# The second layer and the gates by time, the first unit's gates among the first layer's products, and the last pass' fourth head by token halves

## The chip, the cores and the metric

The kernel runs on one NeuronCore of a Trainium2 chip, as one program in one launch. The metric is the device time in microseconds; beside it stands the span, from the first to the last instruction of one profiled execution. Engine names are those of the profile: PE is TensorE's matrix products and PEld its weight loads, DVE is VectorE, ACT is ScalarE, POOL is GpSimd, SP is SyncE, which issues DMAs. The matrix engine writes into PSUM; ScalarE and VectorE read it from there.

## The reference

`x` is 32 x 32 tokens of 256 numbers (batch b, time t), `cond` 32 x 256. Two units are added to x one after the other.

```python
# unit 1: an adaLN block, then a minGRU over time
ada = cond @ ada_w + ada_b                      # shift1, scale1, gate1, shift2, scale2, gate2
x1  = ln(x) * (1 + scale1) + shift1
q, k, v = x1 @ qkv_w + qkv_b                    # 16 heads of 128, attention over the 32 tokens of a batch entry
y   = x + gate1 * (softmax(q k^T / sqrt(128)) v @ out_w + out_b)
h   = gelu((ln(y) * (1 + scale2) + shift2) @ ffn_w1 + ffn_b1)      # 1024 wide
y   = y + gate2 * (h @ ffn_w2 + ffn_b2)
k   = y @ Wz.T + bz ;  n = y @ Wn.T + bn        # gates; the state runs over t:
s_t = (1 - sigmoid(k)) * s_(t-1) + sigmoid(k) * g(n),   s_0 = 0.5 ;   x = x + s
# unit 2: a recurrence over t with drive x, then a sparse MLP
for t in range(32):                             # four Runge-Kutta stages each
    q, p = rk4(q, p, drive=x[:, t])             # dq = q - q^3/3 - p + drive + tanh(q) @ coupling.T + bias
r = q_trace ;  mask = top 4 of 16 blocks of r @ Wr.T + br
x = x + (gelu(r @ W1.T) * mask) @ W2.T
```

## The kernel before

All arrays are held whole in SBUF. Products that need more than half precision are made of f16 pairs, a high and a low part: three products each (high by high, low by high, high by low). ScalarE makes the high part while it empties a PSUM bank, VectorE subtracts and makes the low part, which frees the bank. PSUM is five banks (`bank`), used in turn by a numbered list of uses (`USE_...`; `bank_of` and `count_of` give a use's bank and its turn; `fill` waits for a bank to be free, `full` and `free` are the semaphores), and beside them `score` (two banks) and `spare`.

The program has these stages, and each engine has its own order of work in them, written by hand; the engines meet only in semaphores.

1. *Attention* in four passes of four heads (`attention_pass`). A pass has projections, scores, the mixing of values by the softmax (`mix`, one head each), and output projections (`out_project(pair, c, js)`, c is a quarter of the tokens, js are heads). The softmax of a head is placed as 32x32 blocks on the diagonal of `ptx`: high parts by ScalarE (`place_high`, four strips of 32x256), low parts by GpSimd (`place_low`; in the last pass VectorE has half of those of the fourth head, `place_last_low`). Mixing writes heads into `ao_sb` after `empty_pv` and `low_pv` (`low_last_pv` for the fourth).
2. *The end of the last pass.* When the heads' sums of quarters 0 and 1 are finished, VectorE takes them (`take_heads`), adds them to `acc` (`last_heads`), makes the statistics of the tokens of half 0, and a first part of them is normalised by VectorE, the rest by ScalarE. TensorE turns them (`turn_normed`, `turn_x2`), VectorE scales and shifts (`scale_turned`, `shift_turned`), ScalarE and VectorE make the pair (`x1_high`, `x1_low`). `ada_late` are small products for the modulation. `unread(dst, n)` are n products that nobody reads.
3. *The MLP and the gates.* Tokens are in two halves by batch entry (h is 0 or 1, 512 columns). `hidden_layer(h)` is the first layer, eight uses m of 512 columns, each followed by gelu and a copy on ScalarE and by a difference on VectorE (`hidden_low`). `output_layer(h)` is the second layer, two output blocks ob, 48 products of 512 columns. `residual(h)` adds it to `x3`. `gates(h)` are the f32 products for the minGRU, `min_gru` its recurrence by a scan on VectorE. For h = 1 the gates are split in time already: `EARLY` is t from 0 to 7, `LATE` the rest (`early_gru`, `late_sum`, `late_product`, `late_scan`, `late_drive`). `drive_bias` and `drive_lows` put the result into `drive_pair`, the recurrence's drive. The order on TensorE is hidden_layer(0), output_layer(0), hidden_layer(1), gates(0), output_layer(1), last_gates.
4. *The recurrence.* Eight rounds of four steps of four stages n = 0 to 15. A stage is a chain: ScalarE makes tanh of the state, first in f16 and then in f32, VectorE the low part and the cubic term, TensorE adds drive, coupling and cubic term into `score`, and the next stage's tanh reads it. Beside it TensorE has pieces of the sparse MLP of the group before (`FILL[n]`), unread products (`UNREAD_AT`), ScalarE and VectorE pieces of their own; in round 0 these are the late part of the minGRU (`first_round`), in round 1 its rest (`second_round`). TensorE's rounds are one hardware loop.

TensorE before, between the MLP and the recurrence:

```python
hidden_layer(1)
gates(0)
output_layer(1)
last_gates()
for use in (USE_GRU[1], USE_GRU[1] + 3):
    pe.wait_ge(free[bank_of(use)], count_of(use) + 1)
unread(bank[bank_of(USE_GRU[1])][:], 4)
```

Of the kernel before, what the change touches and what calls it, by code (L numbers as in the profile page):

```python
# [92 lines left out]
def build(nc, xtok, xT, condT, ada_w, vecs, gate_b, out_b, gate_rows, br, wqk, wv, wo, ffn_w1, ffn_w2, wzT, wnT, coupT, wrT, w1T, w2T, out):  # L93
    with ExitStack() as ctx:
# [121 lines left out]
        NE, NL = NBH * 2 * UNROLL, NBH * (T - 2 * UNROLL)  # L216
        parts_at = 2 * MB * P
        early_store = big[:, parts_at:parts_at + KB * 6 * NE].rearrange("p (k w n) -> p k w n", k=KB, w=6)
        parts_at += KB * 6 * NE
# [94 lines left out]
        last_taken = sem("last_taken")  # L314
        pv_full = sem("pv_full")
# [21 lines left out]
        early_full = sem("early_full")  # L337
        early_gate = sem("early_gate")
# [33 lines left out]
        USE_F1 = [[AFTER + n for n in (2, 5, 6, 3, 4, 7, 8, 9)], [AFTER + 3 * KB + MB + m for m in range(MB)]]  # L372
        USE_F2 = [AFTER + 2 * KB + MB, AFTER + 5 * KB + 2 * MB]
        USE_GRU = [AFTER + 3 * KB + 2 * MB, AFTER + 6 * KB + 2 * MB]
# [105 lines left out]
        def _(pool):  # L480
# [23 lines left out]
            for i in range(NQUAD):  # L504
                def place_low(j):

                    if j == QUAD - 1:
                        use = (LAST_PV if i == NQUAD - 1 else USE_PV)[j - 1] + 1
                        pool.wait_ge(full[bank_of(use)], i * NPAR + count_of(use))
                    for q in range(NB4 // 2 if i == NQUAD - 1 and j == QUAD - 1 else NB4):  # L510
# [11 lines left out]
            pool.wait_ge(ptx_ready, NQUAD * QUAD * NB4)  # L522
# [3 lines left out]
        def _(act):  # L526
# [5 lines left out]
            def x1_high(n):  # L532
                h = n % NH
                for k in range(KB):
                    s = slice(h * HALF, (h + 1) * HALF)
                    act.wait_ge(normed, n * KB + k + 1)
                    nc.scalar.activation(x1_pair[:, 0, k, s], drive[:, k, s], ACT.Copy).then_inc(x1_high_ready, 1)  # L537
# [44 lines left out]
            for i in range(NQUAD):  # L582
# [48 lines left out]

                def place_high(j):
# [61 lines left out]
                copy_scores(3, NB4 // 2 if last else NB4)  # L694
                place_high(2)
                exps(3)
                if not last:
                    empty_next_proj(0, 1)
                empty_pv(2, [0])
                place_high(3)  # L700
                empty_pv(2, [1])
                if last:
                    mlp_highs(5, 7)
                else:
                    for t in range(1, 4):
                        weights_high(i + 1, t)
                empty_pv(3)
                if last:
                    mlp_highs(7, 8)
                else:  # L710
# [26 lines left out]

            normalise_x2(0)
            empty_x2(0)
            x1_high(NH)  # L740
            for h in range(NH):
                for m in range(MB):
                    n = h * MB + m
                    if n == MB:
                        normalise_x2(1)
                        mlp_highs(8, 11)
                        x1_high(NH + 1)
                        empty_x2(1)
                        mlp_highs(11, 16)
                    if n >= NGELU:  # L750
                        act.wait_ge(hid_low_ready, n - NGELU + 1)
                    use = USE_F1[h][m]
                    empty(use, gelu_of[n % NGELU], ACT.Gelu, bias=v_("ffn_b1", m), scale=1.0 / WSCALE)
                    act.wait_ge(free[bank_of(use)], count_of(use) + 1)
                    nc.scalar.activation(hid_pair[:, m, 0, h * HALF:(h + 1) * HALF], gelu_of[n % NGELU], ACT.Copy
                                         ).then_inc(hid_high_ready, 1)
            act.wait_ge(coup_ready, 6)
            act.wait_ge(hid_low_ready, NH * MB - 3)
# [10 lines left out]
            def relu_pair(n, piece, cols, ob, src, ready):  # L769

                nc.scalar.activation(nneg_of[n % 2][:, cols], src[:, cols], ACT.Relu, bias=bn_neg[:, ob:ob + 1], scale=-1.0
                                     ).then_inc(gate_in, 1)
                nc.scalar.activation(nn_of[n % 2][:, cols], src[:, cols], ACT.Relu, bias=bn_twice[:, ob:ob + 1], scale=2.0
                                     ).then_inc(ready, 1)
                act.wait_ge(gate_in, piece + 1)
                nc.scalar.activation(nneg_of[n % 2][:, cols], nneg_of[n % 2][:, cols], ACT.Tanh, scale=-0.5
                                     ).then_inc(tn_ready, 1)

            def gate_tanh(n, cols, ob, ready):

                nc.scalar.activation(tz_of[n % 2][:, cols], bank[bank_of(USE_GRU[n // KB] + 2 * ob + 1)][:, cols], ACT.Tanh,
                                     bias=hb[:, ob:ob + 1], scale=0.5).then_inc(ready, 1)

            def wait_product(use):
                act.wait_ge(full[bank_of(use)], count_of(use))

            every = slice(0, HALF)

            for ob in range(KB):
                use = USE_GRU[0] + 2 * ob  # L790
                wait_product(use)
# [1658 lines left out]
```

## Time and profile before

| | us |
|---|---|
| median of 3 runs | 478.56 (478.54 to 478.62) |
| the profiled execution | 478.5 |
| its span | 476.7 |
| PE busy in the span | 464.0 |
| DVE busy | 388.2 |
| ACT busy | 316.9 |
| POOL busy | 47.5 |

The time is that of the whole execution; 1.8 us of it lie outside of the span. Times of the trace count from the first instruction. Attention ends near 228, the first hidden layer starts at 241.4, the recurrence at 300.0. Several engines are busy at once, so shares add up to more than one, and the busy time of matrix products includes the end of each, which overlaps the next one: two products that start 0.22 us apart have 0.38 us each.

### The profile page before, as it was taken

The numbers are of one execution on the slowest core, as the hardware profiler recorded it, in microseconds if no ns is written. First come the engines' busy times: TensorE is split into PE (matmuls) and PEld (weight loads), VectorE is DVE, ScalarE is ACT, GpSimd is POOL, SyncE is SP. The second block draws the span as 40 slices with busy tenths as digits, with TensorE's granted clock in tenths as the row PEclk, the third lists the DMA queues.
The fourth block names the chain that finished last, engine by engine and source line by source line (L and its number), as shares of the span: only waits on it lengthen the run. The fifth ranks groups of instructions, "written<-read, shape, count | busy, mean of one in ns | idle before, by whom it ended". The sixth has DMA issues, their size and how long they took to land.

```text
span 476.7 us, 13783 instructions
## 1 busy us (share of the span) xinstructions
PE 464.0 (97%) x5264; PEld 333.7 (70%) x5264; DVE 388.2 (81%) x1388; ACT 316.9 (66%) x951; POOL 47.5 (10%) x77
## 2 busy tenths in 40 slices
PE   7999999999999999999999999999999999999997
PEld 4455776557755776559635445889898988989886
DVE  4969885869768799998796998898888888888884
ACT  1678873788477965887566974756566656656563
POOL 3010240222120240223000000000000000000000
PEclk9999999999999999999999999999999999999999
DMA  8992511110202000000000000000000000000000
GB/s 288 419 392 71 121 46 36 43 45 23 67 1 66 22 0 2 0 2 1 1 1 1 0 1 0 3 3 1 1 11 1 11 1 11 1 11 12 0 12 23
DMA packets 10400, 20.86 MB, mean 44 GB/s; under 512 B 1472, under 2 KB 4992, under 8 KB 9728
## 3 DMA queue, kind: packets, MB, share of 16 engines
q1 hardware_dynamic: 9808, 19.89, 12.1%
q10 hardware_dynamic: 560, 0.60, 0.4%
q8 instruction: 14, 0.23, 0.2%
q14 instruction: 18, 0.15, 0.1%
HBM read 19.40 MB, written 1.08 MB: 43 GB/s over the span
## 4 chain that ended last, share of the span: by engine, by line
PE 85%; DVE 6%; ACT 4%; DMA 1%; issue 1%; POOL 1%; SPq 0%; DVEq 0%
PE bank L977 57%; PE score L977 26%; PE spare L977 2%; DMA ao_sb<-xtok 1%; POOL ptx L513 1%; ACT ptx L637 1%; ACT th L858 1%; ACT ao_sb L590 1%; DVE drive L1559 1%; ACT x L537 0%; DVE q_group L2310 0%; DVE drive L1563 0%; DVE acc L1651 0%; DVE drive L1714 0%; PE bank L1019 0%
## 5 line engine op out<-in xcount | busy, mean ns | idle before, releaser
L977 PE MATMUL bank<-x,pairs_store 128*128 128x512 f16 x384 | 86.3, 379 | 0.5 <-ACT x L537 0.4
L977 PEld LDWEIGHTS bank<-x,pairs_store 128*128 128x128 f16 x384 | 36.9, 98 | 43.4 <-issue 1.4
L513 POOL TENSOR_TENSOR ptx<-pt,ptx 32x256 f16<-32x256 f32 x62 | 43.2, 696 | 176.3 <-ACT ptx L637 172.9
L977 PE MATMUL score<-cub,neg_eye 128*128 128x64 f32 x256 | 55.6, 299 | 0.0
L590 ACT ACTIVATE big<-bank,head_b 128x512 f16<-128x512 f32 x60 | 39.8, 685 | 17.4 <-PE bank L977 17.1
L2189 DVE TENSOR_TENSOR thlo<-th 128x64 f16<-128x64 f32 x128 | 28.8, 225 | 25.2 <-ACT th L859 23.9
L977 PE MATMUL score<-th,coup_part 128*128 128x32 f16 x1024 | 46.3, 177 | 1.1
L977 PE MATMUL bank<-pairs_store,ao_sb 128*128 128x256 f16 x360 | 43.0, 273 | 0.7 <-issue 0.2
L977 PE MATMUL bank<-pairs_store,x 128*128 128x512 f16 x192 | 43.4, 379 | 0.0
L858 ACT ACTIVATE th<-score 128x64 f16<-128x64 f32 x96 | 21.4, 223 | 32.5 <-PE score L977 29.5
L977 PEld LDWEIGHTS bank<-pairs_store,ao_sb 128*128 128x128 f16 x360 | 34.0, 98 | 7.6 <-DVE ao_sb L1752 1.5
L977 PEld LDWEIGHTS score<-th,coup_part 128*128 128x128 f16 x1024 | 34.6, 96 | 5.5 <-ACT th L858 3.0
L977 PEld LDWEIGHTS score<-cub,neg_eye 128*128 128x128 f32 x256 | 38.1, 188 | 0.0
L977 PE MATMUL bank<-q_high,f_sb 128*128 128x128 f16 x288 | 36.9, 219 | 0.0
L977 PE MATMUL bank<-big,f_sb 128*128 128x128 f16 x456 | 36.3, 219 | 0.2 <-DVE big L2229 0.2
L1752 DVE SCALAR_TENSOR_TENSOR big<-bank,head_b,big 128x512 f16<-128x512 f32 x48 | 33.8, 738 | 0.3 <-ACT big L590 0.2
L977 PE MATMUL score<-thlo,coup_part 128*128 128x32 f16 x512 | 33.5, 179 | 0.3
L977 PEld LDWEIGHTS bank<-pairs_store,x 128*128 128x128 f16 x192 | 18.6, 98 | 21.1 <-issue 0.2
L977 PE MATMUL score<-drive_pair,scaled_eye 128*128 x256 | 31.3, 195 | 1.4 <-issue 0.3
L977 PEld LDWEIGHTS bank<-big,f_sb 128*128 128x128 f16 x456 | 29.2, 101 | 0.5 <-issue 0.3
L588 ACT ACTIVATE big<-bank 128x512 f16<-128x512 f32 x32 | 18.9, 593 | 15.7 <-PE bank L977 15.4
L977 PEld LDWEIGHTS score<-thlo,coup_part 128*128 128x128 f16 x512 | 24.2, 99 | 6.9
(279 smaller groups left out, 1046.7 us busy)
## 6 DMA issues: line engine op xcount, KB each, us to landing
wqk_sb<-wqk SPq DMA_DIRECT2D x16, 256.0 KB, 2.7
wv_sb<-wv SPq DMA_DIRECT2D x4, 512.0 KB, 5.4
wo_sb<-wo SPq DMA_DIRECT2D x4, 512.0 KB, 3.8
f_sb<-ffn_w SPq DMA_DIRECT2D x2, 1024.0 KB, 15.1
ao_sb<-xtok SPq DMA_DIRECT2D x4, 256.0 KB, 5.8
x_sb<-xT SPq DMA_DIRECT2D x1, 1024.0 KB, 12.4
w_sb<-w1T SPq DMA_DIRECT2D x1, 1024.0 KB, 16.0
w_sb<-w2T SPq DMA_DIRECT2D x1, 1024.0 KB, 16.9
```

The lines of the kernel that those rows point to most:

```text
L513: nc.gpsimd.tensor_tensor(ptx[s, 1, :, s], pt[s], ptx[s, 0, :, s], ALU.subtract).then_inc(ptx_ready, 1)
L588: ins = nc.scalar.activation(dst, src, ACT.Copy)
L590: ins = nc.scalar.activation(dst, src, ACT.Identity, bias=bias)
L637: nc.scalar.activation(ptx[s, 0, :, s], pt[s], ACT.Copy).then_inc(high_placed, 1)
L858: nc.scalar.activation(th16[:].rearrange("p (k b) -> p k b", k=KB), src, ACT.Tanh, scale=unit).then_inc(th16_ready, 1)
L977: return nc.tensor.matmul(dst, lhsT, rhs, start=start, stop=stop, **kw)
L1559: V.tensor_tensor(tok(drive[:, k, s]), tok(bank[turned_bank][:]), mod(SCALE1, k, h), ALU.mult).then_inc(free[turned_bank], 1)
L1752: ins = V.scalar_tensor_tensor(lo, bank[bank_of(use)][:], bias, hi, ALU.add, ALU.subtract)
L2189: V.tensor_tensor(thlo[:], th32[:], th16[:], ALU.subtract).then_inc(lo_ready, 1)
```

## The change

*Last pass.* The fourth head's scores, softmax, placing and mixing are done by token halves (`copy_half`, `exps_half`, `place_high_half`, `half_strips`, `shift_half`, `normalise_half`, `mix_half`). TensorE finishes quarters 0 and 1 of all heads first; the second half of the fourth head's mixing and the output projection of quarter 3 come after them, and the last output projections of quarters 2 and 3 go among the turning of the tokens, where unread products were. The modulated tokens of half 0 are written to `centred` instead of `drive`. ScalarE makes x1 before it copies `x3`, and all conversions of the sparse MLP's weights come before the second half's x1.

*MLP and gates.* The first gates of half 0 are made after three of the eight uses of the first layer of half 1, the second ones after all eight. The second layer of half 1 is made for `EARLY` first, into `spare`, both output blocks, then for `LATE`, each block by itself; its residual follows in the same parts, and the early gates stand among the late products of the first block. Of the late gates two products are left before the recurrence, the others are in its stages 0 to 3.

*Recurrence.* Round 0 is written out on TensorE, without logits, second-layer products of a group before and unread products; the loop has rounds 1 to 7. ScalarE's and VectorE's late pieces lie in other stages.

The diff, cut to its core:

```diff
 # TensorE, last pass
+def mix_half(j, h):
+    base = i * (QUAD * NB4) + NB4 * (j + 1)
+    late = j == QUAD - 1
+    pe.wait_ge(high_placed, base + NB4 * h if late else base)
+    dst = score[:, h] if late else fill(use_pv[j] + h)
+    (8 products with the high part of ptx, for the 4 groups of half h)
+    if late:
+        pe.wait_ge(half_placed[h], NB4)
+    else:
+        pe.wait_ge(ptx_ready, base)
+    (4 products with its low part)
 out_project(0, 0, [0, 1])
 out_project(0, 1, [0, 1])
+if last:
+    mix_half(2, 0)
+    mix_half(2, 1)
+    out_project(0, 2, [0, 1])
+    mix_half(3, 0)
+    out_project(1, 0, [2])
+    out_project(1, 1, [2])
+    out_project(1, 0, [3])
+    out_project(1, 1, [3])
+    mix_half(3, 1)
+    out_project(0, 3, [0, 1])
+    return out_project
...
 turn_x2(0)
-ada_late(SHIFT2, fill(USE_F1[0][3]))
-unread(score[:, 0], 3)
+ada_late(SHIFT2, fill(USE_F1[0][0]))
+out_project(1, 2, [2, 3])
+pe.wait_ge(pv_taken, NQUAD * NH)
 turn_normed(0)
-unread(fill(USE_F1[0][4])[:], 8)
+out_project(1, 3, [2, 3])
 # ScalarE, last pass
+copy_half(0)
+copy_half(1)
+place_high(2)
+exps_half(0)
+exps_half(1)
+place_high_half(0)
+empty_pv(2)
+empty_pv(3, [0])
+place_high_half(1)
+mlp_highs(5, 7)
+empty_pv(3, [1])
+mlp_highs(7, 8)
 # VectorE, last pass
-last_strips(3)
-shift(3)
+half_strips(0)
+shift_half(0)
+half_strips(1)
+shift_half(1)
+normalise_half(0)
 low_pv(1, [1])
-normalise(3)
-low_pv(2, [0])
 add_late(SCALE2, spare, 2, 1.0)
-place_last_low()
-low_pv(2, [1])
-low_last_pv()
+normalise_half(1)
+place_last_low(0)
+low_pv(2)
+low_last_pv([0])
+place_last_low(1)
...
 half_var(0)
+low_last_pv([1])
 # TensorE, MLP and gates
+def output_by_time(ob, m, c, dst, times):
+    at = slice(m * D + ob * P, m * D + (ob + 1) * P)
+    steps = hid_pair[:, m, c == 2, HALF:N].rearrange("p (b t) -> p b t", t=T)[:, :, times]
+    return mm(dst, f2_parts[c == 1][:, at], steps, ...)
+def early_output():          # both ob into spare, 24 products of 128 columns each
+def late_output(ob):         # 24 products of 384 columns; early_gates() before m = 5 of ob = 0
+def early_gates():           # waits for x3_ready KB + k + 1 before each k
 hidden_layer(1)              # first_gates(0) stands before its m = AMONG_M = 3
-gates(0)
-output_layer(1)
-last_gates()
-for use in (USE_GRU[1], USE_GRU[1] + 3):
-    pe.wait_ge(free[bank_of(use)], count_of(use) + 1)
-unread(bank[bank_of(USE_GRU[1])][:], 4)
+first_gates(1)
+early_output()
+late_output(0)
+late_output(1)
+pe.wait_ge(x3_ready, 2 * KB + 1)
+late_gate(LATE_N[0], wn_sb, 0, 0)
+late_gate(LATE_Z[0], wz_sb, 0, 0)
+pe.wait_ge(early_gate, 3 * KB)
+unread(score[:, 0], 1)
+mm(score[:, 1], ...).then_inc(seeded, 1)
+pe.wait_ge(x3_ready, 3 * KB)
+late_gate(LATE_N[0], wn_sb, 0, 1)
+late_gate(LATE_Z[0], wz_sb, 0, 1)
 # ScalarE
-for h in range(NH):
-    for m in range(MB):
-...
+for m in range(AMONG_M):
+    hidden_value(1, m)
+act.wait_ge(coup_ready, 6)
+first_gates(0)
+for m in range(AMONG_M, MB):
+    hidden_value(1, m)
+act.wait_ge(hid_low_ready, NH * MB - 3)
+first_gates(1)
 drive_bias(0, 1)
 drive_bias(1, 2)
+(two copies into dropx, before: at n = 6, 7 of round 0)
 early_gates(0)
 early_gates(1)
-late_z(0)
-late_tangent(0)
-late_relu(0)
 drive_bias(2, 3, EARLY)
-late_z(1)
 drive_bias(3, 4, EARLY)
+late_tangent(0)
 # round 0 on ScalarE, before: 0 quarter(0), 1 tangent(1), 2 relu(1), 3 keep(0), 4 quarter(1), 5 keep(1), 10, 11 drive
 # now: 0 relu(0), 1 z(0), 2 quarter(0), 3 keep(0), 4 z(1), 5 tangent(1), 6 relu(1), 7 quarter(1), 8 keep(1), 11, 12 drive
 # VectorE
+for m in range(AMONG_M):
+    hidden_low(1, m)
+first_gru(0)
+for m in range(AMONG_M, MB):
+    hidden_low(1, m)
+first_gru(1)
+early_residual()             # per ob 2 operations of 128 columns
 drive_lows(0, 1)
 drive_lows(1, 2)
-residual(1)
...
-for ob in range(KB):
-    early_gru(ob)
+early_gru(0)
+late_residual(0)             # 2 operations of 384 columns
+early_gru(1)
 drive_lows(2, 3, EARLY)
+late_residual(1)
 # TensorE, recurrence
+for n in range(4 * UNROLL):
+    (at n = 4 and n = 8: waits for the late gates' banks to be free)
+    stage(0, n, [item for item in FILL[n] if item[0] != "logits" and not (item[0] == "out" and item[1] >= 24)], 0)
+    if n < 2:
+        late_gate(LATE_Z[1], wz_sb, 1, n)
+    elif n < 4:
+        late_gate(LATE_N[1], wn_sb, 1, n - 2)
+with pe.Fori(1, T // UNROLL) as i:
+    for n in range(4 * UNROLL):
+        stage(i, n, FILL[n], UNREAD_AT.get(n, 0))
```

## Rows read from the trace of the kernel before

**Rows 1.** The page, part 1: busy time by engine.

```profile
PE 464.0 (97%) x5264; PEld 333.7 (70%) x5264; DVE 388.2 (81%) x1388; ACT 316.9 (66%) x951; POOL 47.5 (10%) x77
```

**Rows 2.** Windows by stage: busy time (count) of PE, PEld, DVE, ACT, POOL, PEclk, DMA, GB/s.

```profile
228.00:241.40 13.40, 11.48 (x78) 7.49 (x77) 11.52 (x30) 6.84 (x12) 0.00 (x0) 1.00 0.00 1
263.70:300.00 36.30, 36.25 (x152) 17.65 (x150) 32.84 (x87) 25.15 (x51) 0.00 (x0) 1.00 0.00 0
```

**Rows 3.** The chain of waits, 229 to 251: start, length, what.

```profile
229.05 0.70 DVE nn_ L1633
...
234.24 1.28 ACT L721
...
237.31 0.70 DVE drive L1708
...
241.44 9.24 PE bank L977 x42
```

**Rows 4.** Timeline, fourth head, then 128-column evictions: start, length, engine, line, operation, count.

```profile
218.67 2.95 POOL L513 TENSOR_TENSOR ptx<-pt,ptx 32x256 f16<-32x256 f32 x4 [4.84 <-ACT ptx L637]
...
222.93 1.71 ACT L637 ACTIVATE ptx<-pt 32x256 f16<-32x256 f32 x4
...
225.27 1.50 PE L977 MATMUL score<-ptx,big 128*128 128x128 f16 x24
...
226.61 1.47 PE L977 MATMUL spare<-pairs_store,ao_sb 128*128 128x256 f16 x12
...
294.03 0.36 ACT L802 ACTIVATE big<-spare,tok_tmp 128x128 f32<-128x128 f32 x1
...
294.28 0.37 ACT L803 ACTIVATE big<-spare,bn_twice 128x128 f32<-128x128 f32 x1
```

**Rows 5.** Timeline, unread products on TensorE before the hidden layer.

```profile
237.04 1.89 PE L977 MATMUL bank<-ptx,scaled_eye 128*128 128x512 f16 x8
```

**Rows 6.** Timeline, TensorE and ScalarE in the second hidden layer and gates.

```profile
261.56 1.23 ACT L537 ACTIVATE x<-drive 128x512 f16<-128x512 f32 x2 [4.64 <-DVE drive L1714]
...
263.69 10.52 PE L977 MATMUL bank<-x,wqk_sb 128*128 128x512 f16 x48
...
269.47 0.67 ACT L715 ACTIVATE npos<-bank,vec 128x512 f32<-128x512 f32 x1
...
270.70 0.67 ACT L715 ACTIVATE za<-bank,vec 128x512 f32<-128x512 f32 x1
...
276.89 0.67 ACT L771 ACTIVATE tn<-bank,bn_neg 128x512 f32<-128x512 f32 x1
...
277.48 1.88 PE L977 MATMUL bank<-ao_sb,wn_sb 128*128 128x512 f32 x4
...
278.55 0.69 ACT L781 ACTIVATE tz<-bank,hb 128x512 f32<-128x512 f32 x1
```

**Rows 7.** Timeline, VectorE from the gates to the recurrence.

```profile
279.36 0.42 DVE L2012 TENSOR_SCALAR za<-tz 128x512 f32<-128x512 f32 x1
...
282.17 0.69 DVE L2024 SCALAR_TENSOR_TENSOR drive<-npos,x_sb 128x512 f32<-128x512 f32 x1
...
287.05 2.42 DVE L2105 SCALAR_TENSOR_TENSOR drive_pair<-drive,c_shifted,drive_pair 128x512 f16<-128x512 f32 x2
...
289.39 0.74 DVE L1998 SCALAR_TENSOR_TENSOR centred<-bank,b_scaled,ada 128x512 f32<-128x512 f32 x1
...
296.46 0.22 DVE L2031 TENSOR_SCALAR big<-big 128x128 f32<-128x128 f32 x1
...
298.21 0.29 DVE L2047 TENSOR_TENSOR drive<-big,x_sb 128x128 f32<-128x128 f32 x1
```

**Rows 8.** Timeline, recurrence: second stage's tanh, then stages 3 and 4 of round 0.

```profile
300.91 0.22 ACT L858 ACTIVATE th<-score 128x64 f16<-128x64 f32 x1 [0.47 <-PE score L977]
...
305.77 0.25 PE L977 MATMUL score<-thlo,coup_part 128*128 128x32 f16 x4
...
305.85 0.60 ACT L841 ACTIVATE big<-big,tok_tmp 128x384 f32<-128x384 f32 x1
306.36 0.20 ACT L858 ACTIVATE th<-score 128x64 f16<-128x64 f32 x1
```

More of the change, by code:

```diff
@@ L739, in _ @@
             empty_x2(0)
-            x1_high(NH)
-            for h in range(NH):
-                for m in range(MB):
[L743 to L756, printed above, removed]
+            for m in range(MB):
+                hidden_value(0, m)
@@ L767, in drive_bias @@
                                      ACT.Identity, bias=c2_shifted[:, ob:ob + 1]).then_inc(drive_high, 1)
[L769 to L787, printed above, removed]
-            for ob in range(KB):
-                use = USE_GRU[0] + 2 * ob
-                wait_product(use)
-                relu_pair(ob, ob, every, ob, bank[bank_of(use)], free[bank_of(use)])
-                wait_product(use + 1)
-                gate_tanh(ob, every, ob, free[bank_of(use + 1)])
+            act.wait_ge(hid_low_ready, NH * MB - 3)
+            first_gates(1)
             drive_bias(0, 1)
             drive_bias(1, 2)
+            for half in range(2):
+                nc.scalar.activation(dropx[:, half * MLP // 2:(half + 1) * MLP // 2], x_sb[:, half, 0:MLP // 2], ACT.Copy
+                                     ).then_inc(dropx_ready, 1)
             def gate_z(ob, z_in, out, done):
@@ L1178, in out_project @@
                         done.then_inc(filled, uses)
+                    elif last and (pair, c) == (0, 3):
+                        done.then_inc(first_heads_out, 1)
                 values(0, 1)
@@ new lines, in first_output @@
+                for c in range(3):
+                    if c == 1:
+                        pe.wait_ge(mlp_split, 8)
+                    elif c == 2:
+                        turn_normed(1)
+                        turn_x2(1)
+                    for m in range(MB):
+                        if c == 0:
+                            pe.wait_ge(hid_high_ready, m + 1)
+                        elif c == 2:
+                            pe.wait_ge(hid_low_ready, m + 1)
+                        for ob in range(KB):
+                            last = part(m, ob, c)
+                            if c == 2 and m == MB - 1:
+                                last.then_inc(full[bank_of(USE_F2[0] + ob)], 1)
@@ new lines, in late_gate, with first_gates @@
+            def late_gate(use, weights, ob, k):
+                dst = fill(use) if k == 0 else bank[bank_of(use)]
+                last = mm(dst[:, 0:NL], weights[:, k, ob * P:(ob + 1) * P], x3_steps[:, k, NBH:B, LATE], k == 0, k == KB - 1)
+                if k == KB - 1:
+                    last.then_inc(full[bank_of(use)], 1)
+            def first_gates(ob):
+                for w, weights in enumerate((wn_sb, wz_sb)):
+                    product(FIRST_GRU[ob] + w, lambda k: weights[:, k, ob * P:(ob + 1) * P], lambda k: x3[:, k, 0:HALF], KB)
@@ new lines, in stage @@
+            def stage(i, n, fillers, unread_count):
+                dst = score[:, n % 2]
+                stages = i * (4 * UNROLL) + n + 1
+                early = EARLY_FILL.get(n, 0)
+                pe.wait_ge(lin_ready, stages)
+                for c in range(2):
+                    mm(dst[:, 0:KB * B], scaled_eye[:],
+                       drive_pair[:, c, bass.ds(i * UNROLL + n // 4, 1)].rearrange("p a n -> p (a n)"), False, False,
+                       skip_group_check=True)
+                pe.wait_ge(th16_ready, stages)
+                for part in coup_parts:
+                    couple(dst, part, th16)
+                fill_in(i, n, fillers[:early])
+                if n % 4 == 0:
+                    subtract_cubic(dst, stages)
+                    pe.wait_ge(lo_ready, stages)
+                    last = couple(dst, coup_parts[0], thlo)
+                else:
+                    pe.wait_ge(lo_ready, stages)
+                    couple(dst, coup_parts[0], thlo)
+                    last = subtract_cubic(dst, stages)
+                last.then_inc(coupled, 1)
+                fill_in(i, n, fillers[early:])
+                for _ in range(unread_count):
+                    mm(bank[NBANK - 1][:, 0:P], scaled_eye[:], scaled_eye[:], True, True)
+                if n == 4 * UNROLL - 1:
+                    pe.wait_ge(h_low_ready, i * MB + MB)
@@ L1937, in _ @@
                                         ).then_inc(first_normed, 1)
+                    add_late(SHIFT2, bank[bank_of(USE_F1[0][0])], 3)
                     take_heads(2)
-                assert own.n == STEPS and pairs[0] == (i + 1) * PAIRS + (0 if last else 4)
-            own.n, own.base = start + NQUAD * STEPS, 0
-            add_late(SHIFT2, bank[bank_of(USE_F1[0][3])], 3)
+                assert own.n == STEPS + (4 if last else 0) and pairs[0] == (i + 1) * PAIRS + (0 if last else 4)
+            own.n, own.base = start + NQUAD * STEPS + 4, 0
             dve.wait_ge(ada2_ready, 5)
```

420 lines of the change are left out of this document (245 added, 175 removed).

## The prediction

> **What bounds the kernel now.** I read the page first: TensorE is busy for 97% of the span [rows 1], so time can come only from TensorE work that goes away, from the 3% of idle, or from work of TensorE's that does nothing. The stage table comes next [rows 2]. The reader should see three kinds of stage. From 228.0 to 241.4 TensorE works 11.5 of 13.4 us, and part of that is on products nobody reads. From 241.4 to 300.0 it works without a gap, with 128x512 products at one per 0.216 us (9.24 us less the last one's 0.38, over 41 steps) [rows 3]. From 300.0 on come eight rounds of 16 recurrence stages; there TensorE looks busy too, but a stage is an exchange TensorE, ScalarE, VectorE, TensorE, some 1.25 us long, so work put beside it is free until it delays the exchange. The chain of waits says what sets the start of the continuous part: VectorE takes the first heads at 229.05, the chain runs over sums, statistics, the load of a table (1.28 us) and the modulation at 237.31, and TensorE is in full flow at 241.44 [rows 3].
>
> **A, the fourth head by halves.** Before, both halves of the fourth head are finished before the first half's last sums are. The change puts second-half work behind them: 12 of the 24 products of the last mixing, at 0.056 us each (1.50 us for 24), and the 12 wide products of quarter 3 (1.47 us) [rows 4]. That is 2.1 us of TensorE time off the way to 229.05. Against it stand waits. The mixing of head 2 by halves waits for GpSimd's last low part (218.67 + 2.95 = 221.62) and gives its first half at 222.1. ScalarE then places four 32x128 strips. No such row exists: 32x256 strips run 0.43 apart (1.71 us for 4) [rows 4], 128x128 evictions 0.25 apart (294.03, 294.28) [rows 4]. I take 0.26, as fixed cost dominates at both sizes; the bounds are 0.25 and 0.43. So 222.15 + 1.1 = 223.25, then two evictions of head 2 to 224.5, the half mixing of head 3 at 224.05 to 224.85, VectorE's low parts of three tiles of 128x512 (0.75 each, as [rows 7] have for one that reads PSUM) to 226.4, the low strips of half 1 to 227.3, and the first heads at 227.35: 1.70 earlier. Behind it one low part (0.75) is put in the chain before the reciprocal, but ScalarE is loading its table there for 1.28 us [rows 3], which hides all but 0.14; without that cover it costs 0.75. The modulation starts at 235.75, 1.56 earlier. The unread products, three and then eight (1.89 us, [rows 5]), go and the two last output projections, 12 products each, take their place: about the same time in the same gaps, so nothing by itself. **A = -1.56**; bounds -1.9 (no wait for GpSimd) and -0.3 (strips at 0.43 on both engines put the first heads at 228.6).
>
> **B, the first unit up to 263.69.** Same products in the same number, so no time. What is moved is six weight splits on VectorE ahead of the second half's modulation, and five conversions on ScalarE ahead of its x1. These end at 258.15 and the modulation would start at 259.63 - 1.56 = 258.07, so they cost 0.1 there; TensorE reaches the second hidden layer at 263.69 when its operands were ready at 262.8 (261.56 + 1.23 [rows 6]), so 0.9 us of cover is there. **B = 0**; bounds 0 and +0.5.
>
> **C, from the second hidden layer (now 262.13) to the recurrence.** TensorE's work: 10.4 us of hidden layer, 6.9 of gates for half 0 (16 passes at (1.88 - 0.59)/3 = 0.43, [rows 6]), split in two now, and the second layer: 48 products of 128 columns (0.056) and 48 of 384 (0.163 by columns) make 10.5 against 48 of 512 at 0.216 = 10.4: no gain. The gain is in order. ScalarE needs 1.24 per hidden value (269.47, 270.70) and 2.35 for a set of gates (276.89 to 279.24) [rows 6]: three values from 265.2, first gates 269.0 to 271.35, five values to 277.6, second gates as their products come (TensorE 262.13 + 10.4 + 6.9 = 279.43) and are done at 280.3. From there VectorE is the bound without a gap. Its rows [rows 7]: the recurrence of the second block 3.5 (279.36 to 282.86), ends 283.9; early residual, four operations of 128 columns at 0.29, 1.2; two drive splits 2.34 (287.05 to 289.39); small fills 0.45, counted the same as now; early recurrence 2.0 (296.46 to 298.21 + 0.29); late residual, two of 384 columns, between the 0.29 of 128 and the 0.75 of 512, say 0.6 each, 1.2; early recurrence 2.0; split of 128 columns 0.4, above a quarter of 1.2 for the fixed part; late residual 1.2. Sum 283.9 + 10.8 = **294.7**, when the last residual is there. TensorE is through the second layer at 291.7, does two late gate products and the seed, and waits here about 1.1 us: this is the new last wait. Then 0.65 for the gate product (two passes, each 384/512 of 0.43), ScalarE's tanh of it 0.46, the first stage's tanh at 296.05, and the first coupling product at 296.35 where before it was at 300.1. That is 3.8; ScalarE then still does the relu of the gate (0.57) ahead of the second stage's tanh, which comes at 297.5 instead of 300.91 [rows 8]: 3.4 earlier, 1.85 of it from C. **C = -1.85**. Bounds: if VectorE's operations of 384 columns last as the 512-column row (0.75) and each hand-over in its run costs 0.05 more, +1.2; if nothing waits and TensorE is the bound, -2.9.
>
> **D, the first round of the recurrence.** Here the removed work comes back. Stages 0 to 3 get a late gate product of 0.65 behind the exchange where 6 to 7 small ones of about 0.35 stood; 0.3 was free, so 0.08 each, 0.3. ScalarE has a late operation of 0.60 in stages 0 to 8, and a drive piece in 11 and 12. At a stage that begins with the four scalings (0.68) this is late: at stage 4 the tanh waited until 306.36 though its sums were there at 306.02 (305.77 + 0.25), 0.3 [rows 8]. New such places are stages 8 and 12, 0.6. Elsewhere it lies in ScalarE's idle between its work for two stages. VectorE: two copies and a fill move from before the recurrence into stage 0 (0.3, hidden, since it waits for ScalarE's late tanh there), one split of 0.54 moves from stage 13 of round 0 to stage 8 of round 1: -0.2 and +0.2. Dropping logits and unread products frees TensorE where it isn't the bound: nothing. **D = +0.9**; bounds 0 and +2.7.
>
> **Sum.** -1.56 + 0 - 1.85 + 0.9 = -2.5. The profiled execution takes 478.5 with a span of 476.7, and the median of the runs is 478.56, the same; so 476.0.
>
> **Waits and queues.** No DMA is added or moved, and SP's queue waits for the same splits as before. GpSimd's last strips wait per half; nothing is behind them. ScalarE and VectorE wait for the last reader of heads 0 and 1 before they write normalised tokens over them; that reader ends near 229.9 and the tokens come at 234, so 4 us of cover. ScalarE's copies of x3 wait for the last output projection (near 237.1) and stand behind x1 now; behind them is the first hidden value, whose sums come at 241.6, after the copies' 1.06 us: no cost. TensorE's wait for the early residual stands inside the second layer (VectorE has its first part at 284.5, TensorE is there at 284.5), with nine products and all of the second output behind it: 0 to 0.3, and the 1.1 us of idle later covers it. [...]
>
> The Trainium skill ("VectorE: DVE Perf Modes", section "The TRN2 errata — SBUF-src ops pay a fixed extra latency per instruction") says that each VectorE or ScalarE instruction carries a fixed cost and advises tiles of 512 and more, which speaks against the halves. Its formula for ScalarE gives, as an estimate by that page, 0.29 us for 128 elements and 0.40 for 256; the trace agrees for the latter with 0.412. By it eight half strips take 2.35 us, where 2.1 is in the sum.
>
> **Rivals.**
> - *Halves cost as much as wholes* (A = -0.3). For it: the 32x256 strips hardly gain on 128x512 tiles (0.43 against 0.63 to 0.69). Against: 128x128 evictions at 0.25 apart. 476.0 + 1.25 = 477.3. Chance 0.12.
> - *A wait takes the place of the gain in C*: TensorE waits for the last residual because VectorE runs as long as it did, each of its operations in that run a little late. For it: VectorE has no slack from 280 on. 0 instead of -1.85: 477.9. Chance 0.13.
> - *Slower: the first round pays for all.* ScalarE's nine gate operations in stages 0 to 8 each delay the tanh by 0.3, as the one at stage 4 did, and the four late gate products delay their stages by their full 0.65: 2.7 + 2.6 = 5.3 against 3.4 gained, 480.4. It decides from D = 3.4. Against: of the six present ones only that at stage 4 delays a tanh. Chance 0.07.
> - *TensorE's clock.* The granted clock is 1.00, the 2.4 GHz level, in every stage [rows 2], also where TensorE worked 11.5 of 13.4 us. The change removes all unread products between attention and recurrence but one and the seed, and those of the first round. If it fell to 1.2 GHz in round 0, the products in the exchange (0.6 us a stage) would double: +9 us, 485. Chance 0.04. The Trainium skill ("TensorE: Matmul & The Clock Gate", part 1) has idle time throttle TensorE's clock, which is this case; no row here shows it.
> - *More gain*: D near 0 and C towards its bound, 474.9. Chance 0.08.
>
> The forecast keeps 0.56, with 475.1 to 477.0 as its own range. 0.2% of this time is 0.96 us, about what a measurement can tell. Faster: 0.56 + 0.08 + 0.07 of the first rival + 0.05 of the second = 0.76; same 0.13; slower 0.11. The range from 474.7 to 478.2 leaves out the slower cases and little else.
>
> **What would show it.** A: VectorE's first take of heads near 227.4, modulation near 235.8. B: second hidden layer at 262.1. C: TensorE idle for about 1 us before a 384-column gate product, released by VectorE's write of the residual; second-stage tanh at 297.5. D: the first round 21.7 to 22.0 us long instead of 21.1, with longer stages at 8 and 12. I am wrong if ScalarE, not VectorE, ends last before the recurrence, if the half strips take over 0.35 each, or if a granted clock below 1.00 appears.

## The result, and the profile after

The median fell from 478.55 to 477.31 us (twelve executions of each), a ratio of 0.9974 with an interval of 0.9964 to 0.9985. The forecast was 476.0: the sign is right, and the gain of 1.24 us is a little under half of the 2.55 forecast. The profiled execution takes 476.61 us with a span of 474.8, so the span shrank by 1.9.

The executions after are not one group. Twenty-four were taken in two sets, and the mean granted clock of TensorE that each shows splits them: 11 at 1.000 with a median of 476.65, 10 at 0.996 with 477.81, 3 at 0.993 with 479.11. The 56 of the kernel before in which the clock was read are all at 0.999 or 1.000 and within 1 us. The trace of after is of the first group, so the missing time falls in two parts: about 0.6 us that the trace must explain (1.9 for 2.5), and 0.7 that it can't show.

Times of two traces compare to some tenths only: in the traces of this kernel and of its later variants the fourth head's first half strip starts between 222.02 and 222.50 us, though nothing ahead of it differs. The two traces compared here, before and after, are close: TensorE's output projections ahead of the fourth head start at 218.41 and 218.34.

Windows of after, with the columns of [rows 2]:

```profile
228.00:241.40 13.40, 10.52 (x87) 7.92 (x86) 11.80 (x30) 7.99 (x14) 0.00 (x0) 1.00 0.00 1
241.40:263.70 22.30, 21.01 (x110) 11.02 (x109) 20.42 (x57) 18.01 (x32) 0.00 (x0) 1.00 0.00 1
```

TensorE is busy for 1 us less between 228 and 241.4 than in [rows 2], and from 241.4 to 263.7, where it was busy for 22.16 us before, it now has 1.3 us of idle. The timeline of after answers to [rows 3, 4] for term A:

```profile
222.14 1.30 ACT L670 ACTIVATE ptx<-pt 32x128 f16<-32x128 f32 x4 [0.84 <-DVE pt L1928]
...
225.75 1.28 ACT L670 ACTIVATE ptx<-pt 32x128 f16<-32x128 f32 x4
...
227.78 0.69 DVE L1748 TENSOR_TENSOR nn_<-bank,drive 128x512 f32<-128x512 f32 x1
...
236.13 0.69 DVE L1825 TENSOR_TENSOR centred<-score,ada 128x512 f32<-128x512 f32 x1 [0.21 <-PE score L1335]
...
240.25 9.24 PE L1028 MATMUL bank<-x,wqk_sb 128*128 128x512 f16 x42 [0.34 <-ACT x L556]
```

The first hidden layer is in full flow at 240.25 where it was at 241.44: 1.19 earlier. The same timeline from there on, and ScalarE's work on the eighth hidden tile:

```profile
249.33 0.97 PE L1028 MATMUL spare<-cond_sb,drive_pair 128*128 128x32 f32 x8
...
250.87 0.67 ACT L762 ACTIVATE var<-bank,vec 128x512 f32<-128x512 f32 x1
...
251.59 3.63 PE L1028 MATMUL bank<-big,wv_sb 128*128 128x512 f16 x16 [1.29 <-ACT var L762]
...
263.71 0.59 PE L1028 MATMUL bank<-x,wqk_sb 128*128 128x512 f16 x2
```

The reader should see the 1.29 us in brackets: TensorE stands ahead of the second layer until ScalarE has emptied the bank of the eighth tile, and the second hidden layer starts at 263.71, where it started before, at 263.69 [rows 6]. All of A is gone there. In the kernel before, the second layer had started ahead of the eighth tile's gelu:

```profile
251.59 3.61 PE L977 MATMUL bank<-big,wv_sb 128*128 128x512 f16 x16
...
252.06 0.67 ACT L715 ACTIVATE var<-bank,vec 128x512 f32<-128x512 f32 x1
```

Then term C, VectorE and TensorE up to the recurrence, and the second stage's tanh, which answers to [rows 7, 8]:

```profile
285.38 0.35 DVE L2147 SCALAR_TENSOR_TENSOR centred<-spare,b_scaled,ada 128x128 f32<-128x128 f32 x1
...
286.56 2.12 DVE L2283 SCALAR_TENSOR_TENSOR drive_pair<-drive,c_shifted,drive_pair 128x512 f16<-128x512 f32 x2
...
294.95 0.56 DVE L2149 TENSOR_TENSOR ao_sb<-ao_sb,centred 128x384 f32<-128x384 f32 x1
...
295.57 0.91 PE L1028 MATMUL bank<-ao_sb,wn_sb 128*128 128x384 f32 x2 [0.32 <-DVE ao_sb L2149]
...
298.33 0.21 ACT L907 ACTIVATE th<-score 128x64 f16<-128x64 f32 x1
```

298.33 for 300.91 is 2.58 earlier. From this tanh to the second one of the next round are 21.93 us in after and 21.33 before: 0.60 goes back. The sum of the trace is -1.19 + 1.21 - 2.60 + 0.60 = -1.98 for a span 1.9 shorter.

### The profile page after: what moved, and what is told of

Its sections match the earlier page's. It is cut to its first block, busy times and chain, and to the rows that moved or that the text cites. A ratio compares the mean times of both kernels' runs of the same rounds, so it can differ in the third digit from the quotient of the medians.

```text
span 474.8 us, 13765 instructions
## 1 busy us (share of the span) xinstructions
PE 458.4 (97%) x5257; PEld 332.6 (70%) x5257; DVE 389.1 (82%) x1402; ACT 317.5 (67%) x958; POOL 47.9 (10%) x79
## 4 chain that ended last, share of the span: by engine, by line
PE 80%; DVE 9%; ACT 6%; issue 2%; POOL 2%; DVEq 0%; POOLq 0%; ACTq 0%
PE bank L1028 51%; PE score L1028 26%; PE spare L1028 2%; POOL ptx L530 1%; ACT th L907 1%; ACT ptx L677 1%; ACT big L794 1%; DVE drive L1674 1%; DVE drive_pair L2283 1%; ACT ao_sb L609 0%; ACT x L556 0%; PE score L1335 0%; DVE q_group L2500 0%; DVE drive L1678 0%; ACT pscaled L916 0%
## 5 line engine op out<-in xcount | busy, mean ns | idle before, releaser
L530 POOL TENSOR_TENSOR ptx<-pt,ptx 32x256 f16<-32x256 f32 x60 | 41.9, 698 | 174.3 <-ACT ptx L677 170.9
L1028 PE MATMUL bank<-big,f_sb 128*128 128x128 f16 x432 | 34.3, 219 | 0.2 <-DVE big L2413 0.2
L1028 PE MATMUL score<-drive_pair,scaled_eye 128*128 (+1 forms) x256 | 30.8, 195 | 1.5 <-DVE score L2576 0.6
L1028 PE MATMUL bank<-q_low,f_sb 128*128 128x128 f16 x144 | 28.3, 218 | 0.0
```

Source lines behind the costliest of these rows:

```text
L1028: return nc.tensor.matmul(dst, lhsT, rhs, start=start, stop=stop, **kw)
```

## The experiments

All ratios are to the kernel before, run on the same chip. The first four ran together, then four, then three. "The clock fell" means a stretch in which the granted clock is 0.50, the 1.2 GHz level; a mean of 0.996 over the span is such a stretch of about 3.4 us, 0.993 one of about 6.8.

**The changed kernel again.** No edit.

> The changed kernel itself, timed again. In twelve runs it lay between 476.44 and 479.33 us with a granted clock between 0.993 and 1.000, while the kernel before kept within 0.9 us. Theory clock: five to seven of ten runs show a clock below 1.000 and are 1 us or more longer, so the median is near 477.3 and the fastest near 476.5. Rival, that the spread belonged to that chip: all runs within 0.5 us, near 476.5.

Measured: 477.71 (476.45 to 479.11), ratio 0.9981 [0.9970, 0.9992]. Its profiled execution, a 477.93, has a mean clock of 0.996, so its trace shows where. Windows of one microsecond, columns as in [rows 2]; the number ahead of the last two is the granted clock:

```profile
309.00:310.00 1.00, 0.75 (x16) 0.63 (x12) 0.93 (x6) 1.00 (x6) 0.00 (x0) 1.00 0.07 16
310.00:311.00 1.00, 0.90 (x16) 0.86 (x17) 0.81 (x6) 0.27 (x3) 0.00 (x0) 0.62 0.00 0
311.00:312.00 1.00, 1.00 (x14) 1.00 (x14) 0.50 (x5) 0.46 (x3) 0.00 (x0) 0.50 0.00 0
...
313.00:314.00 1.00, 1.00 (x21) 1.00 (x20) 0.49 (x4) 0.87 (x4) 0.00 (x0) 0.68 0.00 0
```

From 310.2 to 313.6 TensorE runs at half clock, in stages 9 to 11 of the first round, which last 1.50, 1.78 and 1.64 us where after has 1.22, 1.26 and 1.52: 0.92 us. The rest of the 1.3 us to the trace of after is there before the fourth head, whose first half strip starts at 222.50 for 222.14. Just ahead of the fall, at 308 to 310, TensorE was busy for 1.32 of 2 us. The trace of after has the same 1.32 in the same place (307.64 to 309.64), and its clock stays at 1.00: what TensorE did just ahead doesn't tell the two executions apart.

**The uses exchanged.** The seventh and eighth hidden tiles of the first unit change places.

```diff
-        USE_F1 = [[AFTER + n for n in (3, 4, 2, 5, 6, 8, 9, 7)],
+        USE_F1 = [[AFTER + n for n in (3, 4, 2, 5, 6, 8, 7, 9)],
```

> Uses of the first layer's last two tiles are swapped: the seventh tile goes to the bank that the second layer's first block fills next, and the eighth to another. Theory bank: TensorE's wait of 1.3 us for the eighth gelu before the second layer (it starts at 251.59) goes, the second hidden layer starts at 262.4 to 262.6 instead of 263.71, and all that is behind it comes 1.1 to 1.3 us earlier: span 473.6 with full clock. Rival, that VectorE's six splits before the second half's modulation are then the bound (they end at 258.6, the modulation started at 259.65): the start moves by 0.9 to 1.0 and the rest is lost in a new wait of TensorE for x1; rival two, no change at all, since TensorE would wait at the turning of the tokens.

Measured: 476.17 (475.36 to 477.93), ratio 0.9950 [0.9934, 0.9967]; three of six executions at 1.000, three at 0.996. The fastest is 1.09 below the fastest of the changed kernel. The wait for the eighth tile is gone from the trace: TensorE starts the hidden layer's 42 products at 241.74 and the second layer without a wait at 251.85, 10.11 later, where after has 251.59 - 240.25 = 11.34:

```profile
241.74 9.24 PE L1028 MATMUL bank<-x,wqk_sb 128*128 128x512 f16 x42 [0.34 <-ACT x L556]
...
251.85 3.63 PE L1028 MATMUL bank<-big,wv_sb 128*128 128x512 f16 x16
```

Both start late because the profiled execution is one of those at 0.996, and its fall is elsewhere:

```profile
233.00:233.50 0.50, 0.04 (x2) 0.04 (x2) 0.47 (x3) 0.50 (x1) 0.00 (x0) 1.00 0.00 0
233.50:234.00 0.50, 0.50 (x4) 0.41 (x5) 0.43 (x3) 0.50 (x1) 0.00 (x0) 0.73 0.00 0
234.00:234.50 0.50, 0.50 (x4) 0.35 (x3) 0.47 (x4) 0.49 (x3) 0.00 (x0) 0.50 0.00 0
...
237.00:237.50 0.50, 0.50 (x6) 0.48 (x5) 0.00 (x0) 0.00 (x0) 0.00 (x0) 0.86 0.00 0
```

It lies in the tail of the attention, from 233.7 to 237.1, right behind two waits of TensorE's of 1.0 and 0.5 us. So there are two places, not one. Here too the trace of after has the same two waits (0.95 and 0.46) and keeps its clock. A fall costs more here: the hidden layer is in full flow 1.49 us later than in after, with its half strips 0.12 earlier, so 1.6 us for 3.4 at half clock, where it was 0.92 in the first round.

**Unread products back in the first round.** Ten of 128 columns, in stages 7 and 8, where the other rounds have products of the sparse MLP's second layer that round 0 leaves out.

```diff
-                stage(0, n, [...], 0)
+                stage(0, n, [...], {7: 4, 8: 6}.get(n, 0))
```

> Round 0 of the recurrence gets unread products where second-layer products of a group before were left out: 4 in stage 7 and 6 in stage 8. Theory clock-round-0: the spread of the runs and the clocks below 1.000 go, median 476.5. Rival clock-elsewhere: the same share of runs with a clock below 1.000 as in the changed kernel. Either way a run with full clock takes what the changed kernel takes, within 0.2 us, as these products fit beside the exchange.

Measured: 476.81 (476.58 to 477.06, five executions, all at 0.999 or above), ratio 0.9963 [0.9950, 0.9976]. The fastest is no faster than the changed kernel's; what went is the upper group. With 13 of 24 falling in the changed kernel, five without a fall would come by chance in about 2 of 100. The tail's waits were left as they are, so this run doesn't say that the changed kernel falls there.

**Unread products back at one point of the tail.** Five, behind the last output projection.

```diff
             out_project(1, 3, [2, 3])
+            unread(fill(USE_F1[0][1])[:], 5)
```

> Five unread products of 512 columns stand behind the last output projection, where TensorE waits 1.13 us for the first x1. Theory clock-tail: the spread and the clocks below 1.000 go, median 476.5. Rival: the spread stays. With full clock the time is the same within 0.2 us, as 5 x 0.216 = 1.08 us fit into the wait.

Measured: 477.69 (476.49 to 479.55), ratio 0.9989 [0.9975, 1.0002]; eight of twelve executions at 0.993 or 0.996. No help, against what was expected: these five come behind the place where the fall was seen, and the first round is left open.

**The uses exchanged and the first round's unread products.** Both edits together.

> Bank order of the first unit's last two uses exchanged, so that gelu of the eighth tile no longer holds the bank that the second layer takes, and ten unread products back in stages 7 and 8 of the first recurrence round. Theory (a bank wait of 1.3 us, and TensorE's granted clock falling from 2.4 to 1.2 GHz for some 3.4 us in some executions, at either of two places: about 234 us in the tail of the attention, about 310 us in the first round): fastest runs at 475.4 to 475.8, none with two falls (0.993), some 2 in 10 to 4 in 10 with one fall (0.996) in the tail, 1.2 us longer. Rival (the clock falls in the first round only): every run at 1.000 and within 0.4 us. Rival (the exchange only gained because VectorE had slack, and the unread products cost what it gains): median 476.8.

Measured: one of the six executions took 701.43 us at a mean granted clock of 0.56; it has no trace, its cause is unknown, and it is left out here. The others: 475.63, 475.71, 475.99, 476.87, 477.91; ratio as reported 0.9961 [0.9947, 0.9975]. Two of the five are at 0.996, none at 0.993. The second stage's tanh is at 297.50, 0.83 before that of after. The rival that only the first round falls is out by the trace of the run with the uses exchanged; where the two executions here fell no trace shows.

**The tail filled too.** Eleven unread products more.

```diff
+            unread(fill(USE_F1[0][1])[:], 4)
             turn_x2(0)
             ada_late(SHIFT2, fill(USE_F1[0][0]))
+            unread(fill(USE_F1[0][1])[:], 2)
             out_project(1, 2, [2, 3])
...
             out_project(1, 3, [2, 3])
+            unread(fill(USE_F1[0][1])[:], 5)
```

> As the one before, with eleven more unread products in the tail of the attention, where TensorE waits: 4 before the turning of the sums, 2 behind the modulation's products, 5 behind the last output projection. Theory: no execution shows a clock below 0.999, the runs lie within 0.5 us of each other, median 475.5 to 475.9. Rival (the unread products delay the turning, or the first hidden layer): the second hidden layer starts up to 0.6 us later than without them and the median is 476.2. Rival (the falls come from something other than TensorE's idle time in these two places): clocks of 0.996 as often as before.

Measured: 475.37 (475.16 to 475.92, all at 0.999 or above), ratio 0.9936 [0.9924, 0.9949]. The hidden layer is in full flow at 240.48, where the kernel without them has 240.55: they delay nothing.

**Late pieces moved off the scalings.** ScalarE's second keep from stage 8 to 9, its second drive piece from 12 to 13, in the kernel just told.

```diff
-                elif n == 8:
+                elif n == 9:
                     late_keep(1)
...
-                elif n == 12:
+                elif n == 13:
                     drive_bias(2, 6, LATE, back)
```

> As the one before, with ScalarE's last linear piece of the late gates at stage 9 of the first round in place of stage 8, whose four scalings stand beside it, and the second drive piece at stage 13 in place of 12. Theory: the pair of stages 8 and 9 takes 2.56 us again instead of 2.84, so 0.2 to 0.3 us less than the kernel before it here: median 475.2 to 475.6. Rival (the piece delays whichever stage it stands in): no difference.

Measured: 474.85 (474.66 to 475.31, all at 1.000), ratio 0.9926 [0.9913, 0.9939]: 0.5 less, twice what was expected, since both pieces gave something. Timeline of ScalarE at stage 8, in after and then here:

```profile
308.40 0.68 ACT L916 ACTIVATE pscaled<-ps 128x64 f32<-128x64 f32 x4
308.98 0.60 ACT L897 ACTIVATE big<-big,tok_tmp 128x384 f32<-128x384 f32 x1
309.49 0.20 ACT L907 ACTIVATE th<-score 128x64 f16<-128x64 f32 x1
```

```profile
307.23 0.68 ACT L916 ACTIVATE pscaled<-ps 128x64 f32<-128x64 f32 x4
308.02 0.22 ACT L907 ACTIVATE th<-score 128x64 f16<-128x64 f32 x1
```

The next tanh comes 1.09 us behind the start of the scalings with the piece between them and 0.79 without: 0.30. The same at stage 12 makes 0.60, and from the second tanh to that of the next round this kernel takes 21.37 us, nearly the 21.33 of before.

**The kernel before without its eleven unread products.** Nothing else.

```diff
-            unread(score[:, 0], 3)
             turn_normed(0)
-            unread(fill(USE_F1[0][4])[:], 8)
```

> The kernel before the change, without its eleven unread products between attention and MLP (3 and 8) and nothing else. Theory (these products hold the clock): some runs show a clock of 0.996 and are 1 to 1.5 us above the others, in the profile near 234 to 238 us if the profiled one is among them; the others stay at 478.3 to 478.6. Rival (the tail's clock does not hang on them; the change's other moves made it fall): all runs at 1.000, median 478.4.

Measured: 480.07 (479.37 to 480.70), ratio 1.0035 [1.0022, 1.0048], all five executions at 0.993. TensorE's waits in the tail rise from 0.52 and 0.71 to 1.17 and 2.44 us, and the clock falls there:

```profile
235.00:236.00 1.00, 0.17 (x2) 0.17 (x2) 0.93 (x5) 0.99 (x3) 0.00 (x0) 1.00 0.00 0
236.00:237.00 1.00, 1.00 (x6) 0.51 (x5) 0.83 (x3) 1.00 (x3) 0.00 (x0) 0.71 0.00 0
...
242.00:243.00 1.00, 1.00 (x3) 0.29 (x2) 1.00 (x2) 0.00 (x0) 0.00 (x0) 0.50 0.00 0
243.00:244.00 1.00, 1.00 (x5) 0.44 (x4) 1.00 (x3) 0.00 (x0) 0.00 (x0) 0.87 0.00 0
```

One stretch from 236.4 to 243.3, behind the first of the two waits; the second lies in it. Products that nobody reads are worth 1.6 us here.

**The order of the halves undone.** In the 474.85 kernel, the second half is mixed and quarter 3 multiplied ahead of the first half's last projections.

```diff
+                    mix_half(3, 1)
+                    out_project(0, 3, [0, 1])
                     out_project(1, 0, [3])
                     out_project(1, 1, [3])
-                    mix_half(3, 1)
-                    out_project(0, 3, [0, 1])
```

> One part of the halves undone, in the kernel with the exchanged uses, the unread products and the moved late pieces (474.85): TensorE mixes the second half of the fourth head and multiplies quarter 3 before the first half's last two output projections, as the kernel before the change does; everything else stays by halves. Theory (the order is what the halves gain): VectorE takes the first heads 1.2 to 2.1 us later, the second hidden layer starts as much later, median 476.0 to 476.9. Rival (the gain is in the earlier strips and evictions, and the order is worth nothing since TensorE waits for the strips anyway): within 0.4 us of 474.85.

Measured: 478.04 (477.02 to 480.78), ratio 0.9998 [0.9981, 1.0014]; the six executions at 0.999 or above have a median of 477.19, 2.3 over 474.85. That is more than was expected. VectorE takes the first heads at 230.46 for 227.83, and TensorE then waits 2.36 us at one point:

```profile
233.37 1.04 PE L1028 MATMUL bank<-ptx,scaled_eye 128*128 128x512 f16 x4 [2.36 <-DVE tn L1752]
```

The heads are also 1.4 us later than in the kernel before (229.05): by halves, but in the old order, the last pass is slower than with whole heads, and the new order gives 2.6 of which 1.2 to 1.3 are left as gain. Three executions are at 0.993 and three near 0.996, though the unread products are all there; in the trace, at 0.993, the clock is at half from 234.7 to 241.5. The first four of them stand behind the wait of 2.36, so they don't fill it.

**The 474.85 kernel without the first round's unread products.**

> The same kernel (474.85) without the ten unread products in stages 7 and 8 of the first round, those of the attention's tail kept. Theory (each of the two places has its own fall of the clock, and each is held by its own products): fastest runs 474.4 to 474.8, but some of the runs show a granted clock of 0.996 and 1.0 to 1.4 us more, none 0.993. Rival (the tail's products are enough; the first round fell only as a consequence): all runs at 1.000 and the median 474.6.

Measured: 474.87 (474.73 to 475.96), ratio 0.9933 [0.9920, 0.9946]; one of five executions at 0.996, it is the 475.96. The products cost nothing, and that they matter once the tail is filled rests on this one execution.

**The kernel before with only the change's order of uses.**

```diff
-        USE_F1 = [[AFTER + n for n in (2, 5, 6, 3, 4, 7, 8, 9)],
+        USE_F1 = [[AFTER + n for n in (2, 5, 6, 3, 4, 8, 9, 7)],
```

> The kernel before the change with nothing changed but the uses of the first unit's last three hidden tiles, in the order that the change gives them (8, 9, 7 for 7, 8, 9). Theory (the eighth tile on the bank that the second layer's first output takes is worth its wait, whatever else is changed): TensorE stands some 1.1 to 1.3 us ahead of the second layer, released by the gelu of the eighth tile, and the median is 479.6 to 479.9. Rival (the wait came from the earlier hidden layer, or is covered by the second half's modulation): under 0.4 us, 478.5 to 478.9.

Measured: 479.54 (479.36 to 481.43), ratio 1.0028 [1.0018, 1.0037]: 1.15 slower, slightly under what was expected; one of the ten executions is at 0.996, the 481.43. Its waits of TensorE from 226 to 300 have one that the kernel before hasn't (total, times, longest), and the timeline shows where it stands, then the eighth tile's gelu, the second layer and the second hidden layer:

```profile
PE bank L977 <- ACT rstd L715: 1.0, 1, 1.0
```

```profile
247.66 4.06 PE L977 MATMUL bank<-x,wqk_sb 128*128 128x512 f16 x18 [1.04 <-ACT rstd L715]
...
251.88 0.67 ACT L715 ACTIVATE var<-bank,vec 128x512 f32<-128x512 f32 x1
...
252.61 3.63 PE L977 MATMUL bank<-big,wv_sb 128*128 128x512 f16 x16
...
264.73 1.46 PE L977 MATMUL bank<-x,wqk_sb 128*128 128x512 f16 x6
```

The second hidden layer starts at 264.73 for 263.69: 1.04 of the 1.15. The wait isn't the one that was expected. It stands inside the first hidden layer, ahead of the sixth tile, whose use in this order takes the fourth tile's bank, and it ends when the fourth tile's gelu has read that. The second layer then starts 0.06 us behind the end of the eighth gelu (251.88 + 0.67), without a further wait in the trace. So this run shows that the order of uses alone, without any gate or half moved, costs 1 us; it doesn't show the price of the eighth tile's bank by itself. For that the exchange in the changed kernel stands.

## Why the prediction had the sign and not the size

**A was right in kind and 0.37 too large.** What failed is the size of a half strip: 0.26 us was taken, "as fixed cost dominates at both sizes", and ScalarE places one each 0.33 us (from the start of four to that of its next operation it takes 1.32 and 1.31). Eight of them make 0.56 more, and the first heads came at 227.78 for 227.35, the modulation at 236.13 for 235.75. From there to the modulation it is 8.35 us for 8.26: the low part put into that chain cost 0.09 where 0.14 was forecast. That the order carries this gain is shown by undoing it: 2.6 us at the first heads. My bound from the 32x256 row (0.43) was too dear.

**B failed.** The step was "Same products in the same number, so no time". The products are the same, but their banks aren't. The change gives the eighth tile the use on whose bank the second layer's first output comes next, and that bank is free only when gelu has read the last product of the layer; before, the sixth tile was there, read by 250.25 when the second layer started at 251.59. It cost 1.21 us: 1.29 of wait in the trace, 1.09 between the fastest executions with the uses exchanged. The kernel before, given the same order for its last three tiles, loses 1.15, though by a wait at another tile. It swallowed A, so the 0.9 us of cover that I had put ahead of the second hidden layer never came into play. My list of waits went through queues and semaphores; it lacked which bank each `fill` needs, and who had it last.

**C was right in kind and 0.75 too small.** VectorE sets the end: TensorE waits for its last residual, as forecast, for 0.32 us and not 1.1. From the start of the second hidden layer to that residual I had 294.7 - 262.13 = 32.57 us; it is 295.51 - 263.71 = 31.80. The block's recurrence ends at 21.67 for 21.77, and the run behind it, summed to 10.8, takes from 285.38 to 295.51, 10.13: the two drive splits 2.06 for 2.34, the fills 0.30 for 0.45, the rest a few hundredths each. From the residual to the second tanh are 2.82, forecast 2.8. In the 474.85 kernel the stretch from the second hidden layer to the second tanh is 297.17 - 262.54 = 34.63, in after 34.62: C doesn't depend on when it begins.

**D was 0.9 and is 0.60.** The two new collisions with the scalings, at stages 8 and 12, cost 0.30 each, as read from stage 4 in [rows 8]; moving both pieces by one stage gives nearly all of it back. The late gate products, for which I had 0.3, cost 0.04, as they should by the forecast's own figures (0.65 us each, in the 0.35 of what stood there and 0.3 that were free): stages 1 to 4 take 1.25, 1.31, 1.57 and 1.36 after the change and 1.25, 1.26, 1.54 and 1.40 before.

**Luck.** C and D came out 1.05 us better than forecast, and that hides most of the 1.58 by which A and B were worse; with them as forecast the undisturbed execution would have gained 0.9 us. The measured 477.31 is also what the rival "halves cost as much as wholes" gave (477.3), but its mechanism didn't occur: A is -1.19, not -0.3.

**The clock.** The rival had the mechanism and not the size: I gave it 0.04 and 9 us, for a whole round at 1.2 GHz. It comes in some executions, for 3.4 or 6.8 us, at about 1.2 or 2.5 us of time, and costs the median 0.7. It has a second place, the tail of the attention, which I hadn't counted since TensorE "worked 11.5 of 13.4 us" there, a number that the change itself lowers to 10.52. The unread products that I had costed at nothing were holding the clock: with both places filled none of ten executions fell, with neither 13 of 24, and all five of the kernel before without its eleven. The Trainium skill ("TensorE: Matmul & The Clock Gate", part 1) says that the clock is set by how busy TensorE has been recently; these shares agree.

What stays open: only a trace says in which of the two places the clock fell, and one was taken of each kernel, so how the 13 divide between them isn't known. Nor is what decides, at the same work, whether an execution falls.

**What the change can give.** With the uses exchanged, the waits filled and two late pieces moved, the kernel takes 474.85 us, 0.7% under before and 0.5% under after. It follows the corrected sum to 0.2: -1.19 - 2.60 + 0.04 = -3.75, for a span that is 3.6 shorter (473.1).

## What to carry to other kernels

Where a change renumbers the uses of shared banks, write down for each new use which tile had the bank before and when its last reader is done; count and kind of the products don't tell. Before products that only fill idle time are cut, cost them as what keeps the clock: look at the waits as they stand after the change, put unread products into them and not behind them, and look at the mean clock of every execution, since one trace may be of the undisturbed kind. A small operation on a helper engine is best put in a stage where that engine has nothing else: here one stage further was worth 0.30 us each.

## What the runs showed of the hardware

TensorE's granted clock fell to half behind stretches in which it was far from idle: at 308 to 310 us of the repeated run it had worked 1.32 of 2 us, and with the uses exchanged the two waits in the tail ahead of the fall were 1.0 and 0.5 us. The low stretches seen lasted 3.4 us (310.2 to 313.6, 233.7 to 237.1) or 6.8 us (236.4 to 243.3, 234.7 to 241.5). Of executions of one program some had the fall and some hadn't, with the same 1.32 us of work ahead. The same 3.4 us at half clock cost 0.92 us in the recurrence and 1.6 in the tail. ScalarE's placement on 32 partitions took 0.33 us for 128 elements and 0.43 for 256 [rows 4].
